# 1/sqrt of a LayerNorm split between VectorE and GpSimd, in a reordered opening (S4 and gated FFN block, one core)

## The reference, cut to what matters

```
x  = L0_attn_u                                  # (4, 512, 512) float32
xn = layernorm(x, axis=-1, eps=1e-5)
out = x + s4(xn) + ffn(xn)

ffn:  Wg, Wu, Wd = NF4 codes -> floats, times absmax per block of 64
      g = xn @ Wg.T ; u = xn @ Wu.T             # HD 512 -> M 1792
      return (silu(g) * u) @ Wd.T
s4:   K = kernel of a state space of 64 states, length 512
      return causal_convolution(xn, K) + D * xn
```

## Time and profile before

| | |
|---|---|
| median of 3 runs | 485.91 us (485.49 to 487.23) |
| the profiled execution | 485.5 us, its span 483.4 us |
| TensorE matmul busy | 460.1 us, 95% |
| VectorE busy | 356.6 us, 74% |
| ScalarE busy | 254.3 us, 53% |
| GpSimd busy | 12.3 us, 3%, 46 instructions |

### The profile page before, as it was taken

One profiled execution on the slowest core, in us unless ns is written; L12 is line 12 of the kernel. 1 busy time (PEld: TensorE's weight loads), 2 busy tenths in 40 slices (PEclk: granted clock), 3 DMA queues, 4 the chain that ended last, 5 costly groups with the idle time before them and its releaser, 6 DMA issues.

```text
span 483.4 us, 7048 instructions
## 1 busy us (share of the span) xinstructions
PE 460.1 (95%) x2665; PEld 261.2 (54%) x2665; DVE 356.6 (74%) x595; ACT 254.3 (53%) x411; POOL 12.3 (3%) x46
## 2 busy tenths in 40 slices
PE   0579999999999999999999999999999999999997
PEld 0434444444444444444444464456644588888886
DVE  5989745766666655665555737787899999999993
ACT  5884874766665674444545443684312544544340
POOL 0000070000000000000000000000000000000000
PEclk9999999999999999999999999999999999999999
DMA  8494554322223221211111202237600021011111
GB/s 271 117 234 161 109 119 149 127 67 65 87 77 94 60 76 49 61 46 65 43 45 44 58 31 65 65 90 261 197 0 1 0 88 45 2 45 45 43 45 45
DMA packets 32545, 39.76 MB, mean 82 GB/s; under 512 B 16064, under 2 KB 16256, under 8 KB 32512
## 3 DMA queue, kind: packets, MB, share of 16 engines
q1 hardware_dynamic: 32512, 39.32, 27.4%
HBM read 31.96 MB, written 4.19 MB: 75 GB/s over the span
## 4 chain that ended last, share of the span: by engine, by line
PE 80%; DVE 9%; ACT 1%; DMA 1%; issue 1%; DVEq 0%; ACTq 0%
PE bank L1362 55%; PE bank L1529 20%; PE bank L1476 4%; DVE work L1249 2%; DVE h L1261 1%; DMA xT<-in_x 1%; PE bank L1444 1%; DVE work L773 1%; DVE work L777 0%; DVE work L1254 0%; DVE work L1257 0%; ACT work L551 0%; DVE work L1252 0%; DVE wd L1261 0%; DVE work L1251 0%
## 5 line engine op out<-in xcount | busy, mean ns | idle before, releaser
L1362 PE MATMUL bank<-xT,w 128*128 128x512 f16 (+1 forms) x1260 | 271.0, 377 | 2.6 <-DVE w L783 2.5
L1362 PEld LDWEIGHTS bank<-xT,w 128*128 128x128 f16 x1260 | 122.9, 98 | 149.1 <-ACT yv L649 2.9
L551 ACT ACTIVATE work<-work 128x512 f32<-128x512 int32 x152 | 85.4, 617 | 6.8 <-DMA work<-in_q_gate 3.5
L800 DVE SCALAR_TENSOR_TENSOR h<-bank,sc,work 128x512 f32<-128x512 f32 x42 | 31.4, 750 | 64.0 <-PE bank L1362 61.8
L591 ACT ACTIVATE work<-bank,sc 128x512 f32<-128x512 f32 x56 | 37.9, 681 | 49.4 <-PE bank L1362 48.3
L1529 PE MATMUL bank<-wd,work 128*128 128x256 f16 x504 | 56.2, 273 | 0.4 <-DVE work L1268 0.4
L1529 PEld LDWEIGHTS bank<-wd,work 128*128 128x128 f16 (+1 forms) x504 | 49.2, 98 | 6.6 <-issue 0.9
L563 ACT ACTIVATE work<-work 128x512 f32<-128x512 f32 x41 | 25.6, 625 | 37.9 <-DVE work L764 37.9
L727 ACT ACTIVATE work<-h 128x896 f16<-128x896 f32 x30 | 28.0, 943 | 29.4 <-DVE h L1281 20.5
L1529 PE MATMUL bank<-h,work 128*128 128x256 f16 x378 | 42.2, 273 | 0.0
L1529 PEld LDWEIGHTS bank<-h,work 128*128 128x128 f16 x378 | 37.0, 98 | 4.3
(11 more groups left out here) (132 smaller groups left out, 348.2 us busy)
## 6 DMA issues: line engine op xcount, KB each, us to landing
h<-in_x SPq DMA_DIRECT2D x8, 512.0 KB, 6.0
xT<-in_x SPq DMA_DIRECT2D x16, 256.0 KB, 4.8
out<-xT SPq DMA_DIRECT2D x16, 256.0 KB, 2.0
work<-in_q_gate SPq DMA_DIRECT2D x14, 256.0 KB, 2.7
work<-in_q_up SPq DMA_DIRECT2D x14, 256.0 KB, 2.7
work<-in_am_gate SPq DMA_DIRECT2D x28, 128.0 KB, 2.9
work<-in_am_up SPq DMA_DIRECT2D x28, 128.0 KB, 2.9
work<-in_q_down SPq DMA_DIRECT2D x14, 256.0 KB, 2.6
```

What stands on the lines that cost most here:

```text
L551: nc.scalar.activation(knee_of(u, k), qs[:, u % 2, :], KNEE, scale=scale, bias=bias, alpha=below).then_inc(knee_done, 1)
L800: v.scalar_tensor_tensor(made, up[:], c_up, sil[:, n % 2, :], ALU.mult, ALU.mult).then_inc(h_done, 1)
L1362: mm = nc.tensor.matmul(out_b, weights(k)[:, unit, wl, f, :], xT[:, TPC * c + first:TPC * c + last, xl, f, :], start=(i == 0), stop=(i == ...
```

## The change

1. **Groups of the 1/sqrt.** VectorE's `rstd(i)` covers tiles 0 to 3 only. Chunks 1 to 3 are done on GpSimd, by a function of 17 operations in 15 dependent steps, each chunk once its four moments are there. ScalarE's normalisations of tiles 4 and up wait for it.
2. **Normalisation.** All 16 tiles on ScalarE; the two on VectorE are gone.
3. **Turning.** Tiles 6 and 7 are turned by TensorE like chunk 0 (banks 6 and 7), between unit 2 and unit 3 of chunk 0; only tiles 4 and 5 of chunk 1 go through the DMA transpose. The four warm-up matmuls before the first product are gone.
4. **Units 2 and 3.** Unit 3 uses the second set of side buffers, and the steps of units 0 to 3 are interleaved. The knees of units 2 and 3 come after the normalisation of chunk 0 but for two of unit 2.
5. **Loads.** Tile 0 of x goes first, alone, ahead of the first codes, then tile 1 alone; absmax loads move up.
6. **Order.** All engines' opening lists are rewritten; the small products for B stand after unit 1.

```diff
+        def rstd_rows(a, b):
+            return ([mv[:, a:b, 1]] + [rs[:, k, a:b] for k in (0, 1, 2, 3, 6)]), rs[:, 4, a:b], rs[:, 5, a:b]
...
         def sides_of(u):
-            return (acc_1[:, 0, :], acc_1[:, 1, :]) if u == 1 else (acc_l, acc_r)
+            return (acc_1[:, 0, :], acc_1[:, 1, :]) if u in (1, 3) else (acc_l, acc_r)
...
-        FIRST_STEPS = [(0, RIGHT), (0, LEFT), (0, WHOLE), (1, RIGHT), (1, LEFT), (1, WHOLE), (0, SCALED), (1, SCALED)]
+        FIRST_STEPS = [(0, RIGHT), (0, LEFT), (1, RIGHT), (0, WHOLE), (1, LEFT), (0, SCALED), (1, WHOLE), (2, RIGHT),
+                       (1, SCALED), (2, LEFT), (2, WHOLE), (3, RIGHT), (2, SCALED), (3, LEFT), (3, WHOLE), (3, SCALED)]
...
+            sp.dma_start(xs[:, 0, :], x_v[:, 0, :]).then_inc(x_ld[0], 16)
             load_codes(0, q_gate[0])
-            load_x(0)
+            sp.dma_start(xs[:, 1, :], x_v[:, 1, :]).then_inc(x1_ld, 16)
             load_x(1)
             load_codes(1, q_up[0])
...
-            for t in range(4, 8):
-                turn(t)
+            turn(4)
+            turn(5)
...
+            def rstd(c):                                           # GpSimd
+                (var, hv, y, p, r, ys), scale, bias = rstd_rows(TPC * c, TPC * c + TPC)
+                at = RSTD_NEXT * (c - 1)
+                pool.wait_ge(mv_done, TPC * c + TPC)
+                pool.tensor_scalar(y, var, EPS, None, ALU.add).then_inc(rs_next, 1)
+                pool.tensor_scalar(bias, mv[:, TPC * c:TPC * c + TPC, 0], -1.0, None, ALU.mult).then_inc(rs_next, 1)
+                pool.wait_ge(rs_next, at + 1)
+                pool.tensor_scalar(ys.bitcast(I32), y.bitcast(I32), -0.5, float(RSQRT_MAGIC),
+                                   ALU.mult, ALU.add).then_inc(rs_next, 1)
...
+                pool.wait_ge(rs_next, at + 15)
+                pool.tensor_tensor(scale, p, ys, ALU.mult).then_inc(rs_next, 1)
+                pool.wait_ge(rs_next, at + 16)
+                pool.tensor_tensor(bias, bias, scale, ALU.mult).then_inc(rs_next, 1)
+
+            for c in range(1, NCH):
+                rstd(c)
...
             def norm(t):                                           # ScalarE
-                act.wait_ge(rs_step, RSTD if t < 8 else RSTD * (t // TPC))
+                if t < TPC:
+                    act.wait_ge(rs_step, RSTD)
+                else:
+                    act.wait_ge(rs_next, RSTD_NEXT * (t // TPC))
...
-                    if u >= 2:
-                        dve.wait_ge(wlo_done, u)
+                        dve.wait_ge(wlo_done, u - 1 if u < 4 else u)
...
-            warm_up(4)
...
             product(0, 0, 2, TPC).then_inc(gate_done, 1)
+            products(0, (1,))
             pe.wait_ge(s4_ld, 48)
...
-            products(0, (1,))
             products(1, (0,))
+            turn(6)
+            turn(7)
             pe.wait_ge(b_cp, 1)
             products(1, (1,))
```

More of the change, by code:

```diff
@@ L625, in _ @@
             clamp(1)
[L626 to L629, removed]
+            make_knee(2, 2)
+            make_knee(2, 3)
+            for t in range(TPC):
+                norm(t)
             x_hi(0)
@@ L660, in _ @@
             clamp(5)
+            norm(8)
             h_hi(1)
-            norm(8)
+            x_hi(8)
             weight_hi(5)
-            x_hi(8)
             norm(9)
@@ L671, in _ @@
             silu(2)
+            knees(6)
             silu(3)
-            knees(6)
             clamp(6)
@@ L956, in _ @@
             x_lo(1)
-            items(10, 11)
+            step(1, SCALED)
+            stats(6)
             x_lo(2)
+            stats(7)
+            moments(4, 8)
             x_lo(3)
+            step(2, LEFT)
             weight_lo(1)
-            items(11, 12)
+            step(2, WHOLE)
+            step(3, RIGHT)
             scales(9)
-            items(13, 14)
+            step(2, SCALED)
+            step(3, LEFT)
             scales(10)
-            items(14, 15)
+            weight_lo(2)
@@ L966, in _ @@
+            step(3, WHOLE)
+            stats(8)
+            step(3, SCALED)
             x_lo(4)
-            items(15, 16)
-            weight_lo(2)
             x_lo(5)
-            items(16, 17)
-            x_lo(6)
-            items(18, 19)
-            x_lo(7)
-            items(19, 20)
             scales(11)
             weight_lo(3)
+            x_lo(6)
             scales(12)
-            items(20, 22)
+            x_lo(7)
+            stats(9)
+            items(20, 21)
+            stats(10)
@@ L1000, in _ @@
-            rstd(1, 7)
-            rstd(1, 8)
-            items(28, 29)
-            rstd(1, 9)
-            rstd(1, 10)
-            rstd(1, 11)
-            items(29, 30)
+            items(21, 22)
+            h_lo(0)
+            items(23, 25)
+            h_mul(1)
+            items(25, 27)
+            weight_lo(4)
+            h_lo(1)
+            items(28, 30)
+            x_lo(8)
+            weight_lo(5)
+            x_lo(9)
             stats(12)
-            weight_lo(5)
-            x_lo(8)
+            x_lo(10)
@@ L1010, in _ @@
             stats(13)
-            x_lo(9)
+            x_lo(11)
             stats(14)
-            x_lo(10)
             stats(15)
-            x_lo(11)
+            moments(12, 16)
             h_mul(2)
-            moments(12, 16)
-            rstd(2, 0)
-            rstd(2, 1)
-            rstd(2, 2)
             h_mul(3)
-            for i in range(3, 6):
-                rstd(2, i)
             items(30, 31)
-            for i in range(6, 9):
-                rstd(2, i)
             items(31, 32)
-            for i in range(9, 12):
-                rstd(2, i)
@@ L1421, in _ @@
                     bank_free(n)
+                if c == 1:
+                    pe.wait_ge(xlo_done, 8)
                 if c > 0:
[L1423 removed]
+                    pe.wait_ge(xt_ld[c], 16 * (2 if c == 1 else TPC))
                 products(n)
```

191 lines of the change are left out of this document (98 added, 93 removed).

## The result

The change makes the kernel slower: 491.72 us in the median of four runs (490.8 to 493.73), against 486.57 (485.49 to 487.86) of before beside it; ratio 1.0119, 95% interval 1.0093 to 1.0144. The forecast was 491.3, with 5.4 us added; measured are 5.2. How that sum came about is another matter: several terms of it were off and cancelled.

A forecast was written before the change was run, and what follows sets the result against it. Opening changes were taken to move TensorE's later products one for one, with VectorE and ScalarE nearly full behind it. Terms -2.1, +5.0, +2.0 and +0.5 sum to +5.4 us, giving 491.3 us; range 483.6 to 494.

The forecast's parts named there:

- steps 1 to 4: Opening through unit 3 of chunk 0: reordered loads, normalisation and transposes save 2.1 us if GpSimd is on time.
- step 5: Chunk 1's 1/sqrt on GpSimd, stretched beside VectorE's two-SBUF-operand operations, makes TensorE wait at tiles 6 and 7: +5.0 us.
- step 6: Chunk 2's 1/sqrt on GpSimd, stretched likewise, delays unit 5's weights and makes TensorE wait: +2.0 us.
- step 7: Chunk 3's 1/sqrt on GpSimd makes the last four DMA transposes about as late as their slack: +0.5 us.
- Step 1: First loads: codes behind 256 KB of x, first knees at 4.5 us, unit 1's still at 8.1; cost nothing.
- Step 2: Chunk 0's opening: first product at 18.9 us instead of 22.07; losing the warm-up matmuls costs nothing.
- Step 3: First product's second half waits for x_lo of tile 3, ending at 22.2 us; TensorE idles 2.0 us.
- Step 4: Tiles 6 and 7 turned on TensorE in 1.9 us; unit 3's weight wait of 2.48 us disappears.
- A: GpSimd's 1/sqrt groups finish on time, so steps 5 to 7 fall away: 483.8 us; chance 20%.
- B: GpSimd stretched half as much; TensorE waits 2 to 3 us at tile 6, gain used up: 486 us; chance 7%.
- C: GpSimd's identity matrix 2 us late, delaying the whole opening: 485.8 us without contention, 493.3 with it; chance 5%.

The follow-up runs named there:

- the version with the gain: Changed kernel with all 1/sqrt on VectorE, the old load order and four warm-up matmuls restored: 485.56 us, ratio 0.998; run again 485.45 us, ratio 0.9978.
- The filler run: Changed kernel plus 28 filler matmuls of 256 columns, result unused, on TensorE before the transposes of tiles 6 and 7: 490.98 us, ratio 1.0099.

## Why the prediction was right in sum, and where not in its terms

| term | forecast, us | measured, us, and where |
|---|---|---|
| steps 1 to 4 | -2.1 | -0.2: all 1/sqrt on VectorE against before; +0.6 in the traces and at equal clock |
| step 5, chunk 1 on GpSimd | +5.0 | +4.2: changed kernel against chunk 1 on VectorE; some 1.7 of it is the clock |
| step 6, chunk 2 | +2.0 | +0.5: chunks 2 and 3 together 1.3 (487.56 to 486.25), less chunk 3 |
| step 7, chunk 3 | +0.5 | +0.8: chunk 3 alone |
| sum | +5.4 | +5.3, of 5.2 measured between the kernels |

The third column takes differences of medians, some of them from different groups of runs; each is good to about one microsecond. Its sum agrees by the way it is taken, step by step from the changed kernel back to before, and is no proof of the terms. That the total was hit is luck: steps 1 to 4 came out 2 to 3 us too hopeful, steps 5 to 7 together 2 us too dear, and these cancelled.

- *Step 1 failed.* "Unit 1's still at 8.1, with the same bytes ahead": 10.56. The same bytes took longer with tile 1 in a piece of its own, as the run with one piece shows.
- *Step 2 failed in its size, and by its own mark.* First product 20.77, not 18.9 and "not before 20". Tile 1 was late and so the moments (11.1 for 9.0); from there to the product it took about as long as forecast. That the loss of the warm-up costs nothing held, but the reason given did not: the clock column said 1.00 while the work ran at half pace.
- *Step 3 was right in kind:* the second half waits for tile 3, until 23.9 (forecast 22.2). Its wait is only 0.44, since TensorE's own slow start fills the rest.
- *Step 4 was right:* the 2.48 is gone in every version with the new opening; at full clock its transposes are even cheaper than the 0.24 each of the earlier trace rows, 0.60 for four.
- *Of the -2.1 nothing came that shows.* With all 1/sqrt on VectorE the first product starts 2.0 late (20.92 for 18.9), its second half 1.9 (24.08 for 22.2), and two waits of 0.6 follow, one for unit 2's weights and one for tile 7: the 60 matmuls begin at 34.23 where 31.7 was forecast. The loads are one part: undoing them (and adding the warm-up) brings the product of 58.04 to 56.41. The -2.1 also presumed VectorE without chunk 1's twelve steps and a GpSimd on time. As no run has both, what the relief of VectorE would be worth was not measured and stays open.
- *Step 5 was right in mechanism and nearly in size:* 9.1 us for the seventeen where 9.5 were forecast (21.6 to 31.1), ScalarE idle 4.75 for 5, TensorE 3.78 and 0.72 for 4.5 and 0.7. It left out what came with the wait: 1.2 GHz from about 35 to 41.5 us, +1.7 on the 60 matmuls. Longest single operation 1.75, where 1.2 stood.
- *Step 6 was a wait that was there but did not count.* Its 2.0 assumed that TensorE arrives on time at 55. Behind chunk 1's wait and the half clock, it arrived just as the weights did. Where TensorE was on time, it waited 2.40 (before with chunks 2 and 3 on GpSimd) or 1.51; where it was a little late (the run with four warm-up matmuls), 0.75. The forecast added terms that overlap. Chunk 2 was never moved alone, so the +0.5 is only a difference.
- *Rivals.* A is refuted by the profile after, where GpSimd is done at 32.46 and not before 26, and B by TensorE's 4.5 us at tiles 6 and 7. C is half there: the identity matrix came last in several runs and moved by 0.8 us between two runs of one kernel (TensorE's first matmul at 11.62 and 10.85, both released by it), but it does not decide the sign.

## What to carry to other kernels

Work moved to GpSimd is free for VectorE and may take twice its time there while VectorE's stream has two SBUF sources: place it only where nobody waits for it, or give it twice the time. A stop of TensorE can cost more than its length: here the matmuls behind one of 2.4 us or more often ran slower for a few microseconds. When delays are added up along one chain, ask of each later one whether the earlier delay has already covered it. Before you credit a gain of half a per cent to an edit, compare the executions at the same mean clock.

## What the runs showed that was not expected

- The clock column and the pace disagree at the start. The stretches before TensorE's first long piece of work show 1.00, yet the first twelve matmuls took 2.72 us in every version without warm-up, and 1.47 to 2.15 with four ahead. The pace of the rows is what counts there.
- The float32 transposes show the same. Four take 1.12 us at tile 7, at a shown clock of 0.50, and 0.60 with it at 1.00 (in the version with the gain, at 30.86). The sixteen of the opening take 3.67 in the earlier trace rows, 0.23 each, which is nearer to the lower level's pace (1.12 for four, 0.28 each) than to the full one's (0.15 each), under a column that says 1.00. The forecast read this 0.24 as the full one.
- What makes the clock fall was not found; these rows narrow it. A wait of about 2.4 us was followed by full clock in the profiled execution of before (2.48, then 60 matmuls in 13.11, behind 7.5 us of work without a stop) and by half clock in two others: with the low halves moved (2.41, then 12 in 4.06, behind 7 us nearly without a stop) and in the run with chunks 2 and 3 on GpSimd (2.40, then 36 in 9.63, behind 15.7 us). So neither the wait's length nor the work ahead of it decides alone.
- The same kernel does not always do the same. In the five versions whose traces show no wait over 1.7 us behind the first product (the new opening with chunk 1 on VectorE, but for the low halves moved; 69 executions) the mean clock is always 0.999 or 1.000. It is that in 36 of the 76 executions of before, in 6 of the 12 with the low halves moved, in 1 of 12 with chunks 2 and 3 on GpSimd, and in none of the four of the changed kernel. The filler run shows that short waits do not ensure it: its longest is 1.18, and it is 1 of 4 there.
- GpSimd's first real operation starts between 8.9 and 11.8 us, whatever the edit, after 8 to 11 us of idleness that no row explains; the cause was not found.
